# Three layer norms rebuilt: a token's factor by Newton steps, and the norm behind linear attention without activation tables

## The reference

```python
x = x + 0.5 * L0_ffn(layernorm(x))    # top-2 of 8 experts, silu(g) * u, plus a shared expert
x = x + L0_attn(layernorm(x))         # 4 blocks of linear attention, each with two norms and a gelu FFN
x = x + 0.5 * L0_ffn(layernorm(x))
x = x + 0.5 * L1_ffn(layernorm(x))    # expert choice, below
x = x + L1_attn(layernorm(x))         # causal softmax attention, 16 heads of 8
x = x + 0.5 * L1_ffn(layernorm(x))

def layernorm(x, eps=1e-05):
    m = mean(x); v = var(x)           # over the 128 features
    return (x - m) / sqrt(v + eps)

def L1_ffn(x):                        # x: 8 x 256 x 128, 8 experts, k = 64 tokens per expert and sequence
    scores = einsum('ntd,ed->nte', x, gate_w)
    probs = softmax(scores, axis=-1)
    g, m = top_k(probs.transpose(0, 2, 1), k)
    h = gelu(einsum('nekd,edf->nekf', x[batch, m], w1))
    return zeros.at[batch, m].add(g[..., None] * einsum('nekf,efd->nekd', h, w2))
```

## Time and profile before

| what | us |
|---|---|
| median of 3 runs | 1140.3 |
| lowest and highest run | 1140.15, 1151.54 |
| the profiled execution | 1144.14 |
| its span in the profile | 1142.4 |

### The profile page before, as it was taken

One profiled execution on the slowest core, in us unless ns is written; L12 is line 12 of the kernel. 1 busy time (PEld: TensorE's weight loads), 2 busy tenths in 40 slices (PEclk: granted clock), 3 DMA queues, 4 the chain that ended last, 5 costly groups with the idle time before them and its releaser, 6 DMA issues.

```text
span 1142.4 us, 12658 instructions
## 1 busy us (share of the span) xinstructions
PE 954.2 (84%) x4387; PEld 637.8 (56%) x4395; DVE 672.9 (59%) x1247; ACT 626.3 (55%) x986; POOL 349.1 (31%) x257
## 2 busy tenths in 40 slices
PE   6899997599999998689999974998567777675998
PEld 4678884233333333257888852886344554443797
DVE  2888885567777877437888826242645545226222
ACT  5455554378888887645555554445342544443443
POOL 1597775000000000006777725201011121204300
PEclk8999998789999999969999987999768877775999
DMA  5225110000000000033122101100000000001001
GB/s 162 40 83 155 58 66 8 0 1 1 1 1 0 1 1 1 0 97 73 64 64 65 47 1 55 38 1 1 1 2 3 3 3 2 2 1 37 1 1 37
DMA packets 30932, 33.61 MB, mean 29 GB/s; under 512 B 2254, under 2 KB 19990, under 8 KB 30870
## 3 DMA queue, kind: packets, MB, share of 16 engines
q1 hardware_dynamic: 30870, 32.82, 10.0%
HBM read 31.36 MB, written 1.18 MB: 28 GB/s over the span
## 4 chain that ended last, share of the span: by engine, by line
PE 63%; DVE 20%; ACT 10%; POOL 3%; issue 3%; DMA 0%; SPq 0%; ACTq 0%; DVEq 0%; POOLq 0%
PE ps L122 10%; PE ps L123 9%; PE ps L124 9%; PE ps L595 5%; PE ps L732 5%; DVE smax L1697 3%; PE ps L753 2%; PE ps L589 2%; PE ps L814 2%; PE ps L487 2%; PE ps L573 2%; ACT L1139 2%; ACT ex L1258 2%; PE ps L493 2%; PE ps L704 2%
## 5 line engine op out<-in xcount | busy, mean ns | idle before, releaser
L1800 POOL TENSOR_TENSOR fl<-fp,fh 128x512 fp32r<-128x512 f32 x144 | 225.6, 1588 | 128.5 <-ACT fh L1062 128.4
L1053 ACT ACTIVATE fs<-ps 128x512 f32<-128x512 f32 x144 | 86.2, 599 | 115.6 <-PE ps L124 115.3
L1396 DVE TENSOR_TENSOR fp<-fp,cwb 128x512 f32<-128x512 f32 x128 | 139.0, 1086 | 13.7 <-DVE fp L1389 0.5
L1389 DVE TENSOR_TENSOR fp<-fs,ps 128x512 f32<-128x512 f32 x144 | 98.1, 682 | 38.8 <-ACT fs L1053 37.6
L122 PE MATMUL ps<-z_hi,w_hi 128*128 128x512 f32 x288 | 116.7, 405 | 3.4 <-DVE fp L1389 3.3
L123 PE MATMUL ps<-z_lo,w_hi 128*128 128x512 f32 x288 | 115.7, 402 | 0.0
L124 PE MATMUL ps<-z_hi,w_lo 128*128 128x512 f32 x288 | 114.1, 396 | 0.0
L1062 ACT CAST fh<-fp 128x512 fp32r<-128x512 f32 x144 | 88.8, 617 | 34.7 <-DVE fp L1396 30.2
L1865 POOL TENSOR_TENSOR ln_sq<-ln_rs 128x512 f32<-128x512 f32 x20 | 21.1, 1056 | 272.8 <-ACT ln_rs L1102 272.8
L1858 POOL TENSOR_SCALAR_AFFINE_SELECT ex<-ex 128x1024 f32<-128x1024 f32 (+1 forms) x24 | 33.7, 1403 | 171.8 <-ACT ex L1258 171.8
L1697 DVE TENSOR_REDUCE smax<-ps 128x8 f32<-128x2048 f32 (+1 forms) x24 | 55.0, 2291 | 34.0 <-PE ps L828 27.3
(11 more groups left out here) (245 smaller groups left out, 2021.7 us busy)
## 6 DMA issues: line engine op xcount, KB each, us to landing
cwb<-cw_spread SPq DMA_DIRECT2D x64, 256.0 KB, 3.2
w_raw<-in_L_ffn_w_dram SPq DMA_DIRECT2D x20, 256.0 KB, 3.1
w_raw<-in_L_ffn_w_dram SPq DMA_DIRECT2D x4, 512.0 KB, 6.2
w<-in_L_ffn_w_dram SPq DMA_DIRECT2D x8, 256.0 KB, 5.4
x_tok<-in_L_attn_x_dram SPq DMA_DIRECT2D x4, 256.0 KB, 3.9
wb<-in_L_attn_W_dram SPq DMA_DIRECT2D x1, 1024.0 KB, 7.1
wb<-in_L_attn_W_dram SPq DMA_DIRECT2D x4, 256.0 KB, 4.1
stk<-mT SPq DMA_DIRECT2D x64, 4.0 KB
```

The lines of the kernel that those rows point to most:

```text
L1053: act.activation(fs[:, n % 2, :], ps[:, n % 2, :], ACT.Silu).then_inc(silu_done, 1)
L1389: dve.tensor_tensor(f, fs[:, n % 2, :], ps[:, 2 + n % 2, :], ALU.mult).then_inc(prod_done, 1)
L1396: dve.tensor_tensor(f, f, cwb[:, x % CW_RING, :], ALU.mult).then_inc(weighed, 1)
L1800: pool.tensor_tensor(fl[:, n % RING0, :], fp[:, n % RING0, :], f32(fh[:, n % RING0, :]), ALU.subtract).then_inc(flo_done, 1)
```

## The change

Three norms are taken out of the routine: `LN_FFN0B`, `LN_FFN1` and `LN_FFN1B`. `LN_FFN0` and `LN_ATTN1` keep it.

- The variance of a token becomes one column: a matmul with 128 tokens of the square as the weights and one column of 1/128 as the moving operand gives the 128 variances on the partitions, four such matmuls per block (`ln_variance`). DVE makes the inverse root `ln_r` from them by a seed from the bits of the number and three Newton steps (`ln_root`, 11 operations on at most 128x16). Ln, Exp and their two table loads go.
- Ahead of `ffn1` the centred block, not the normed one, is copied to `z` (`ln_copy`). Gate scores and turned tiles are made from it. DVE multiplies the scores by the token's factor ahead of the softmax, and ACT applies the factor as the scale of four copies per block when it evacuates the turned tokens, then rounds from SBUF.
- Ahead of the second `ffn0` the factor is spread over the partitions by four matmuls per block (`ln_spread`: the factor's column, broadcast, as weights, the identity as the moving operand), and DVE multiplies the centred copy by it (`ln_scale`). Halves as before.
- The steps are moved: centring, squares and variances of the first blocks stand inside the end of the stage before (`attn0`, the last downs of `ffn0`, the last sequence of `attn1`), and the gate scores of `ffn1` stand behind that stage too. The first up of `ffn0` stands ahead of all logits in its second call.
- Banks are assigned anew: `XT1, SC1` become (5, 6, 7, 0) and 4; the last block's turn and projection in `attn1` use banks 6 and 7.

The diff at its core:

```diff
+ROOT_SEED = 1597463007.0
+ROOT_STEPS = 3
...
+            def ln_centre(n, tb):
+                pe.wait_ge(ln_in, NTB * n + tb + 1)
+                pe.matmul(ps[:, LN_BANK[n][tb], :], centre[:], blk(xr, tb), start=True, stop=True).then_inc(lxc_ready, 1)
+
+            def ln_variance(n, tb):
+                pe.wait_ge(lsq_ready, later(n, tb))
+                for q in range(TPB):
+                    c = tb * TPB + q
+                    ins = pe.matmul(ps[:, LN_VAR[n], c:c + 1], ln_sq[:, tb, q * P:(q + 1) * P], mean_w[:, 0:1], start=True, stop=True)
+                ins.then_inc(lvar_ready, 1)
+
+            def ln_spread(n, tb):
+                pe.wait_ge(root_ready, later(n, tb))
+                pe.wait_ge(lxc_copied, later(n, tb))
+                for q in range(TPB):
+                    ins = pe.matmul(ps[:, LN_BANK[n][tb], q * P:(q + 1) * P], ln_r[:, tb, q:q + 1].broadcast_to([P, P]), ident[:],
+                                    start=True, stop=True)
+                ins.then_inc(spread_ready, 1)
...
-                logits(0)
-                up(0)
+                if call == 1:
+                    for tb in range(NTB - 1):
+                        ln_spread(ln, tb)
+                    ln_variance(ln, NTB - 1)
+                    pe.wait_ge(z_ready, u0 + 1)
+                    up(0)
+                    ln_spread(ln, NTB - 1)
+                    logits(0)
...
                     down(n)
+                    if call == 1 and n == ALL0 - 4:
+                        ln_centre(LN_FFN1, 0)
+                        ln_centre(LN_FFN1, 1)
+                    if call == 1 and n == ALL0 - 3:
+                        ln_centre(LN_FFN1, 2)
+                    if call == 1 and n == ALL0 - 2:
+                        ln_variance(LN_FFN1, 0)
+                        ln_variance(LN_FFN1, 1)
+                if call == 1:
+                    ln_variance(LN_FFN1, 2)
+                    ln_centre(LN_FFN1, NTB - 1)
+                    for tb in range(NTB - 1):
+                        scores(LN_FFN1, tb)
+                    ln_variance(LN_FFN1, NTB - 1)
+                    scores(LN_FFN1, NTB - 1)
...
+                for tb in range(NTB - 1):
+                    ln_centre(LN_FFN0B, tb)
+                for tb in range(NTB - 1):
+                    ln_variance(LN_FFN0B, tb)
                 for t in range(NTB):
                     pe.wait_ge(a0_vector[t], V0("z2", NBLK - 1))
+                ln_centre(LN_FFN0B, NTB - 1)
...
                     if s >= 1:
+                        if s == SEQS:
+                            ln_variance(LN_FFN1B, 0)
+                            ln_variance(LN_FFN1B, 1)
                         pe.wait_ge(causal_done, 3 * s)
...
+                    if s == SEQS - 1:
+                        ln_centre(LN_FFN1B, 0)
+                        ln_centre(LN_FFN1B, 1)
                 turn(NTB - 1)
+                ln_centre(LN_FFN1B, 2)
                 project_out(NTB - 1)
+                scores(LN_FFN1B, 0)
+                ln_variance(LN_FFN1B, 2)
+                ln_centre(LN_FFN1B, NTB - 1)
+                scores(LN_FFN1B, 1)
+                scores(LN_FFN1B, 2)
+                ln_variance(LN_FFN1B, NTB - 1)
+                scores(LN_FFN1B, NTB - 1)
...
-                    act.copy(xtf[:, tb % 2, :], ps[:, XT1[tb], :]).then_inc(xtf_done, 1)
-                    act.copy(xt_hi[:, tb * TPB:(tb + 1) * TPB, :], ps[:, XT1[tb], :].rearrange("p (q d) -> p q d", d=P)).then_inc(xth_done, 1)
+                    for q in range(TPB):
+                        ins = act.activation(xtf[:, tb % 2, q * P:(q + 1) * P], ps[:, XT1[tb], q * P:(q + 1) * P], ACT.Copy,
+                                             scale=ln_r[:, tb, q:q + 1])
+                    ins.then_inc(xtf_done, 1)
+                    act.wait_ge(xtf_done, t + 1)
+                    act.copy(xt_hi[:, tb * TPB:(tb + 1) * TPB, :], xtf[:, tb % 2, :].rearrange("p (q d) -> p q d", d=P)).then_inc(xth_done, 1)
...
+            def ln_root(n, first, last):
+                v, r, t = (x[:, first:last + 1, :] for x in (ln_v, ln_r, ln_t))
+                dve.wait_ge(lvar_ready, later(n, last))
+                own.did(dve.tensor_scalar(v, ps[:, LN_VAR[n], first * TPB:(last + 1) * TPB].rearrange("p (b q) -> p b q", q=TPB),
+                                          EPS_OUT, None, ALU.add))
+                own.wait()
+                own.did(dve.tensor_scalar(r.bitcast(I32), v.bitcast(I32), -0.5, ROOT_SEED, ALU.mult, ALU.add))
+                own.wait()
+                for step in range(ROOT_STEPS):
+                    own.did(dve.tensor_tensor(t, r, r, ALU.mult))
+                    own.wait()
+                    own.did(dve.scalar_tensor_tensor(out=t, in0=t, scalar=-0.5, in1=v, op0=ALU.mult, op1=ALU.mult))
+                    own.wait()
+                    ins = dve.scalar_tensor_tensor(out=r, in0=t, scalar=1.5, in1=r, op0=ALU.add, op1=ALU.mult)
...
+                if call == 1:
+                    ln_root(ln, 0, 2)
+                    ln_scale(ln, 0)
+                    ln_scale(ln, 1)
+                    ln_low(ln, 0)
+                    ln_scale(ln, 2)
+                    ln_root(ln, 3, 3)
+                    ln_low(ln, 1)
+                    ln_low(ln, 2)
+                    ln_scale(ln, 3)
                 product(0)
+                if call == 1:
+                    ln_low(ln, 3)
...
+                dve.wait_ge(root_ready, later(ln, NTB - 1))
+                own.did(dve.tensor_tensor(sce[:], ps[:, SC1, 0:TILES * EXP].rearrange("p (t e) -> p t e", e=EXP),
+                                          ln_r[:].rearrange("p b q -> p (b q)")[:, :, None].broadcast_to(full), ALU.mult))
                 own.wait()
```

More of the change, by code:

```diff
@@ L9 @@
 U32 = mybir.dt.uint32
+I32 = mybir.dt.int32
 ALU = mybir.AluOpType
@@ L509, in layer_norm, with scores @@
                 norm_parts(u0, src, busy)[1]()
+            def ln_centre(n, tb):
[14 more added lines that the diff above has]
+                ins.then_inc(spread_ready, 1)
+            def scores(n, tb):
+                pe.wait_ge(lxc_copied, later(n, tb))
+                for t in range(tb * TPB, (tb + 1) * TPB):
+                    ins = pe.matmul(ps[:, SC1, t * EXP:(t + 1) * EXP], z[:, t * P:(t + 1) * P],
+                                    par[:, COL_GW:COL_GW + EXP], start=True, stop=True)
+                if tb == NTB - 1:
+                    ins.then_inc(sc_ready, 1)
             def ffn0(call, ln):
@@ L664, in ffn1 @@
                 for tb in range(NTB):
[L665 to L670, removed]
+                    pe.wait_ge(lxc_copied, later(ln, tb))
                     for q in range(TPB):
@@ L1047, in ffn0 @@
                 act.preload_act_table_set("silu_and_others")
+                if call == 1:
+                    ln_square(ln, NTB - 1)
+                    ln_copy(ln, NTB - 1)
+                    for tb in range(NTB - 1):
+                        ln_high(ln, tb)
                 def gate(n):
@@ L1078, in ffn0 @@
                     gate(n)
+                    if call == 1 and n == 0:
+                        ln_high(ln, NTB - 1)
                     if n == 1:
@@ L1087, in ffn0 @@
                 high(ALL0 - 1)
+                if call == 1:
+                    ln_square(LN_FFN1, 0)
+                    ln_square(LN_FFN1, 1)
+                    ln_square(LN_FFN1, 2)
+                    for tb in range(NTB - 1):
+                        ln_copy(LN_FFN1, tb)
+                    ln_square(LN_FFN1, NTB - 1)
+                    ln_copy(LN_FFN1, NTB - 1)
+                    act.preload_act_table_set(LN_EXP)
             def attn0():
@@ L1167, in attn0 @@
                         fed(*rd)
+                for tb in range(NTB - 1):
+                    ln_square(LN_FFN0B, tb)
+                for tb in range(NTB - 1):
+                    ln_copy(LN_FFN0B, tb)
             def ffn1(call, ln):
@@ L1340, in layer_norm, with ln_scale, ln_low @@
                 low(NTB - 1)
[L1342 to L1345, removed]
+            def ln_root(n, first, last):
[12 more added lines that the diff above has]
+                    ins = dve.scalar_tensor_tensor(out=r, in0=t, scalar=1.5, in1=r, op0=ALU.add, op1=ALU.mult)
+                    if step < ROOT_STEPS - 1:
+                        own.did(ins)
+                        own.wait()
+                ins.then_inc(root_ready, last + 1 - first)
+            def ln_scale(n, tb):
+                dve.wait_ge(spread_ready, later(n, tb))
+                dve.tensor_tensor(blk(z, tb), ps[:, LN_BANK[n][tb], :], blk(z, tb), ALU.mult).then_inc(y_done, 1)
+            def ln_low(n, tb):
+                dve.wait_ge(zh_done, NTB * HALVED.index(n) + tb + 1)
+                dve.tensor_tensor(blk(z_lo, tb), blk(z, tb), f32(blk(z_hi, tb)), ALU.subtract).then_inc(z_ready, 1)
             def ffn0(call, ln):
```

90 lines of the change are left out of this document (61 added, 29 removed).

## The result

The kernel after takes 1132.5 us (median of 12 runs, 1129.1 to 1137.8). The kernel before, run 12 times beside it, took 1144.4, 4.1 above the median of the three runs that the prediction started from. The ratio is 0.990, 95% interval 0.9885 to 0.9923: the change wins 9 to 13 us. The prediction said 1124.8 in a range of 1112 to 1134, and a gain of 15.5.

A forecast was written before the change was run, and what follows sets the result against it. The prediction took PE, with 63% of the span on the chain, and the serial chains around three norms as the bound. Gains 5.2 + 8.0 + 2.3 = 15.5 us from 1140.3 gave 1124.8, range 1112 to 1134.

The forecast's parts named there:

- A: Norm behind linear attention, ahead of the second ffn0 (top-2 FFN), up to its second up matmul: gain 5.2 us.
- C: Norm ahead of the second expert-choice FFN (ffn1), from the last attention outputs to the turned probabilities: gain 2.3 us.
- B: Norm ahead of the first expert-choice FFN (ffn1), from the last down matmul to the turned probabilities: gain 8.0 us.
- wrong as a whole: Signs against the forecast: dense work behind a stage at 0.50 for 10 us more, or B gaining under 5.
- half from the spreads on: Case in A: spreads and everything after at 1.2 GHz, logits ending at 506.2; gain 3.6 us.
- full until variance 3, then half: Case in A: 2.4 GHz through block 3's variance, then 1.2 GHz, logits ending at 503.05; gain 6.8 us.
- scores 0-2 and variance 3 at full: Term in B: three gate-score blocks and the last variance at 2.4 GHz, 3.8 us, ending at 671.1.
- All half from the scores: Case in B: everything from the gate scores on at 1.2 GHz; gain 5.3 us.
- full throughout: Case in C: 2.4 GHz from 1005.4 to the end of the stage; gain 7.9 us.
- Full clock: Rival: earlier centres and filled gaps hold 2.4 GHz through all three stages; gain 27.0, 1113.3 us; chance 0.12.
- Half clock: Rival: without wide variance matmuls every stage soon runs at 1.2 GHz; gain 6.7, 1133.6 us; chance 0.18.
- The cold stretches behind the stages: Rival: thin work leaves following dense work longer at 1.2 GHz; 20 us each gives 1154.8 us; chance 0.05.

The follow-up runs named there:

- run 12: Not a label of a run: the words say that the kernel before was measured 12 times beside the kernel after; 1144.4 us.
- e1: The kernel before plus three unused 64-byte tiles where the change puts its small tiles, no instruction differing; 1152.4 us, ratio 1.0075.
- e2: The kernel after with its three small tiles moved to the end, so all other tiles start where they did before; 1124.4 us, ratio 0.984.
- e6: e2 with one more unused tile of 64 bytes a partition behind `eps`; one run at 1132.1 us.
- e7: e2 with one more unused tile of 256 bytes a partition behind `eps`; one run at 1128.5 us.
- e5: The kernel after with only the norm ahead of the second ffn0 put back to the tables; 1139.8 us, ratio 0.9957.
- e8: e2 with 13 unread wide matmuls in PE's wait for the top-k and one ahead of the first gather, both ffn1 calls; 1120.0 us, ratio 0.9758.
- e4: The kernel after with 32 columns in each variance and score matmul, the extra ones not read; 1129.8 us, ratio 0.9887.
- e9: e8 with 32 columns in each variance and score matmul, the extra ones not read; 1114.4 us, ratio 0.9727.
- e3: The kernel after with eight unread wide matmuls in PE's wait for the top-k, both ffn1 calls; 1131.6 us, ratio 0.990.

## Why the prediction came out as it did

The predicted time was 7.7 too low. 4.1 of that is the base: the three runs had a lower median than the twelve. The other 3.6 is the gain, 11.9 by medians where 15.5 was forecast. In the profiles it is 10.5: two more from the stages, seven less from the rest. That the time still fell within 1112 to 1134 is in part luck: A and C won 5.6 more than forecast and so covered the 3.7 that B won less, and the forecast's own range, 1119.5 to 1129.5, missed it. "Faster", by its line of 1%, had a chance of 0.72; the ratio, 0.990, lies on that line. Of the prediction's own signs the last down of B (1.8 later), the outputs of C (5.3 later) and the Newton chain came as said, but one of those for "wrong as a whole" came too: B gained 4.3, under 5.

*"What follows each of the three ends does the same work before and after, so I carry a new schedule to each end and subtract."* This step failed. The work was the same, its speed was not. Three small tiles in front of the others lengthened every matmul step of ffn0 by 3 to 4 ns (e1, e2, e6, e7), a cost that stands in no row of before and that I had no term for: the diff's lines on allocation are part of the change. And the stretches with the gathers and the first ups got longer by 4.2 in the two calls together; the first gathers ran at 0.51 in after and at 0.64 before.

*A, 5.2; measured 7.3* (6.7 between e5 and after). The schedule up to the root was right to 0.1 us (start 486.44, end 488.66; forecast 486.37 and 488.7). I had weighed "half from the spreads on" and "full until variance 3, then half", one fall in each. The clock was at 0.50 in the spreads and back at 1.00 behind them. A spread at half was 5.49/3 = 1.83; I had taken the wide matmul's 1.70.

*B, 8.0; measured 4.3.* The order of the steps held: centre 3 started 7.2 behind the start of centre 0, forecast 7.56 from the end of down(68). The term that failed is "scores 0-2 and variance 3 at full", 3.8: they took 4.92 + 1.70 = 6.6, since the clock fell as centre 3 began, and the root and the scores behind it waited; centre 3 itself took 1.93 for 0.86. All half from the scores, 5.3, was thus still too much. With the tiles in their old places the same steps took 3.5 and B won 8.6 (e2), so that this miss too goes with the addresses.

*C, 2.3; measured 5.8.* The outputs took 2.8, forecast 3.0. The term that failed is half clock from the last turn on: it was 1.00 up to 1012, so that the projection, scores 0, variance 2 and centre 3 were still done at full. In e2, e8 the same stage won 3.6, in e4 8.0, just past my "full throughout".

*Prices.* The Newton chain was 2.2 (forecast 2.3), a thin block 0.79 to 0.90 at full (0.95) and 1.70 at half (1.62). The cover for ACT's turned copies held: they and their casts ended at 680.2 (forecast near 682), gathers came at 690.1.

*Rivals.* Full clock did not come by itself, though PE was busy for all of 664 to 674 in after. In e4, e8 and e9 more of it was had; from after to e9 the medians fall by 18 (1132.5 to 1114.4), 8 of them already from after to e2. Half clock described B in after, not A and C. The cold stretches behind the stages, the slower rival, were real but 4.2 us in all, far from the 15.5 at which they decide.

## What to carry to other kernels

A new tile, however small, moves all that is declared after it: put it behind the others, or fill up to the old alignment (here by 256 bytes), and compare the matmul step of an untouched dense stretch first. When a serial stage on PE is shortened, its remaining matmuls are priced by the clock they meet, so forecast with both prices for each piece and let the range carry it. Where PE must wait ahead of dense work and a bank is free, wide matmuls that nobody reads are worth trying; in e3 they ended 5.3 us too early and won nothing.

## What the runs showed of the hardware that I had not expected

- The step of back-to-back float32r matmuls of 512 columns, at a granted clock of 1.00 and with PE never idle, was 228.9 to 229.1 ns or 231.8 to 232.6 ns, by whether the starts of the tiles behind `eps` were moved by 0 or 256 bytes a partition, or by 64 or 192.
- PE was at work for all of 3.20 us of 3.20 in e8, and for 10.00 of 10.00 in after, at a granted clock of 0.50.
- Variance matmuls with 32 columns were no dearer at full clock than with 1: two blocks, 16 instructions, took 1.68 with 1 column in after, and 1.70 with 32 in e4:

```profile
659.04 1.70 PE ps L538 x16
```
